# A two-layer transformer block on one core: hand-written entry lists for layer two's units 0 to 3, and the first expert-weight transfers beside slots 0 to 3

## The chip, the cores and the metric

The kernel runs on one core of one Trainium2 chip. The metric is the device time of one execution in microseconds; lower is better. The engines are TensorE (PE in the profile), VectorE (DVE), ScalarE (ACT), GpSimd (POOL) and SyncE (SP), each with an in-order list of instructions; they meet at semaphores.

## What is computed

The input x has 128 sequences of 64 tokens, 128 features each. Cut to its core, the reference is:

```python
x = x + tanh(g_xattn[0]) * xattn0(layernorm(x), ctx, ctx)   # 16 heads, mask by blocks of 32 keys
x = x + tanh(g_ffn[0])   * ffn0(layernorm(x))               # top-1 of 8 experts, gelu, 128 -> 512 -> 128
x = x + tanh(g_xattn[1]) * xattn1(layernorm(x), ctx, ctx)   # 16 heads, causal, key padding
x = x + tanh(g_ffn[1])   * ffn1(layernorm(x))
# ffn1: 16 experts, gates w = softmax over the active ones of (cosine(x, sim) - sigmoid(gates))
#   q, k, v = sum_e w_e * (x @ proj_e);  o = softmax(q k^T / sqrt(128)) v
#   out = sum_e w_e * (o @ o_proj_e)
```

## The kernel before, in words

The 8192 tokens are 32 units of 256 tokens (four sequences, two tiles of 128). Four stages follow each other: layer one's attention with its router, unit by unit (to about 384 us of the profile); the routing, which clears the padding rows and builds the slot table (384 to 398); layer one's experts, 71 slots of 128 sorted tokens (398 to 544); and layer two, attention and dense experts together (from 546 on).

Each engine's work is a list written out by hand. In layer two `body1(u)` is one step of the pipeline on each engine: it does the dense experts of unit u, the attention of unit u+2 (scores, maxima, subtraction, exponentials, transposes of the probabilities `upper_probs`, products with the values `upper_weigh`, heads, output), queries, keys and values of unit u+3 and the norm and first transposes `upper_in` of unit u+4. `upper_units` (L326) runs it for u = -5 to 33, so that for u below 0 only the parts of units that exist are there. The attention of unit 0 is thus in body1(-2) and that of unit 1 in body1(-1), one after the other in the same order as in the steady state. The step for u = 0 is the first with dense parts (L1758 to L1760, `part`).

What the change touches, with its lines:

- SP: `zero_rows` (L380) loads four row numbers into registers and then issues four transfers of zeros into `sorted_in`; ACT runs it too, for the other four experts. `load_slot` (L460) brings the rows of a slot. `load_context` (L488) brings a unit's stored context columns into `xcT`. `place_keys` (L404) spreads the keys `kT` into `kx` with four transfers.
- POOL: `gather` (L570) fetches a unit's tokens from `sorted_out` with two indirect transfers; `norm` and `second_norm` (L593 to L596, `deviation`) turn mean and variance into scale and shift; `pad_row` (L584, L587) makes a unit's mask; `add_part` (L718) adds the dense experts' parts.
- ACT: `apply_norm` (L812), `copy_xT` (L768), `keys` (L776), `queries` (L784), `copy_v` (L793), `exp_bank` (L911), `copy_pT` (L830), `copy_oT` (L837), `copy_hidden` (L918), `gate_exp` (L943), and `load_rows` (L892), which issues the transfers of the dense experts' weights `proj_raw`, two experts and one of q, k, v, o at a time.
- DVE: `first_stats` and `second_stats` (L1058 to L1062), `max_bank` (L1318), `normalise` (L1095, L1097), `add_residual` (L1104), and the gates (L1260 to L1310).
- PE: `upper_in` (L1853), `upper_queries_keys` (L1862 queries, L1863 keys), `upper_values` (L1523), `upper_scores` (masks L1887, products L1549), `subtract_bank` (L1896), `upper_probs` (L1569), `upper_weigh` (L1584), `upper_heads` (L1844), `upper_output` (L1872), `upper_normed` (L1819) and `gate_products` (L1827).

`upper_in`, `upper_values`, `upper_heads`, `upper_normed` and `gate_products` share the bank m0; queries, keys and output share m1; `since` names the semaphore after which the bank's earlier user is done.

Of the kernel before, what the change touches and what calls it, by code (L numbers as in the profile page):

```python
# [7 lines left out]
ACT = mybir.ActivationFunctionType  # L8
# [8 lines left out]
P = 128  # L17
# [9 lines left out]
RING0 = 6  # L27
# [50 lines left out]
def flamingo(nc, a, out):  # L78
    ctx = ExitStack()
    with ctx:  # L80
# [144 lines left out]
        with ExitStack() as first:  # L225
            def sb_first(name, shape):
# [60 lines left out]
                  "hn_lo_ready", "oh_lo_ready", "qk1_in_psum", "qk1_ready", "s1_in_psum",  # L287
# [38 lines left out]
        def upper_units(eng, body):  # L326

            for u in range(-5, UNITS + 2):
                body(u)
# [50 lines left out]
        def zero_rows(eng, experts):  # L380

            eng.wait_ge(routed["zero"], 1)
            rows = [eng.value_load(padi[0:1, e:e + 1], min_val=0, max_val=E0 * REGION - P) for e in experts]
            for row in rows:
                eng.dma_start(sorted_in[bass.ds(row, P), :], zrow[:, :]).then_inc(routed["padded"], 16)
# [5 lines left out]
        def _(sp):  # L391
# [78 lines left out]
            rows = [row_of(sl) for sl in range(2)]  # L470
            sp.wait_ge(routed["padded"], 16 * E0)
            for par in range(2):
                sp.wait_ge(scattered[par], 16 * UNITS)
            for sl in range(RING0):
                load_slot(sl, sl, rows[sl] if sl < 2 else row_of(sl))
            slots(sp, slot)

# [12 lines left out]

            def store(v):
# [10 lines left out]

            upper_units(sp, body1)
# [5 lines left out]
        def _(g):  # L509
# [228 lines left out]

            upper_units(g, body1)
# [3 lines left out]
        def _(act):  # L743
# [26 lines left out]
            def keys(layer, v):  # L770
                q = s[layer]
                if exists(v):
                    act.wait_ge(q["qk_in_psum"], v + 1)
# [102 lines left out]
            act.activation(warm[:, :], eps[:, :], ACT.Gelu)  # L876
            act.wait_ge(routed["table"], 1)
# [17 lines left out]

            def load_proj(i, n):
# [5 lines left out]
            for n in range(4):  # L902
                load_rows(slice(0, 2), n)
            slots(act, slot, load=load_proj)
# [100 lines left out]

            upper_units(act, body1)
# [3 lines left out]
        def _(v):  # L1010
# [437 lines left out]

            upper_units(v, body1)
# [3 lines left out]
        def _(pe):  # L1453
# [236 lines left out]
            ins.then_inc(setup["table_in_psum"], 1)  # L1690
            pe.wait_ge(routed["table"], 1)
# [164 lines left out]
            def upper_queries_keys(v):  # L1856

                if exists(v):
                    since((v - 4, f["qk1_ready"], v - 3), (v - 2, s[1]["x_mid_ready"], v - 1), (v - 1, s[1]["k_ready"], v))
                    pe.wait_ge(s[1]["xcT_ready"], v + 1)  # L1860
                    pe.wait_ge(ctx_loaded[1][v % 2], 8 * (v - v % 2 + 2))
                    pe.matmul(m1[:, 0:256], wq[1][:, :], xcT[v % 2][:, 0, :], start=True, stop=True)  # L1862
                    pe.matmul(m1[:, 256:512], wk[1][:, :], xcT[v % 2][:, 1, :], start=True, stop=True)\  # L1863
# [137 lines left out]
```

## Time and profile before

| | us |
|---|---|
| median of 3 runs | 1701.73 (1701.27 to 1704.68) |
| profiled execution, its own time | 1705.36 |
| its span from first to last instruction | 1703.6 |
| TensorE busy over the span | 1599.9 (94%) |
| last slot's output issued, first gather of layer two | 543.8, 546.4 |
| first dense part of layer two (L1758) | 601.5 |

The profile counts an instruction as busy between its start and its end; a row of the timeline gives start, duration, engine, line, operation, and in brackets how long the engine had been idle and what ended that. The chain of waits is followed back from the last instruction, so that each piece in it is what the end waited for. The granted clock of TensorE is written as a share of 2.4 GHz: 1.00 is 2.4 GHz and 0.50 is 1.2 GHz.

### The profile page before, as it was taken

What the parts mean: (1) busy time and instruction counts of PE and PEld (TensorE: products, weight loads), DVE (VectorE), ACT (ScalarE), POOL (GpSimd) and SP (SyncE); (2) the same over time, 40 slices, a digit from 0 to 9 for tenths busy, and PEclk for the clock granted to TensorE, in tenths of its full rate; (3) what the DMA queues carried; (4) which work ended last, traced back from release to release, by engine and by line L of the source; (5) the groups of instructions that cost most, each with busy time, mean ns of one, the idle gap of its engine ahead of it and who ended that gap; (6) DMA issues with size and microseconds to landing.
All of it is one profiled execution on the core that took longest, in us unless ns stands there. A gap on an engine that the chain in (4) does not pass through costs nothing.

```text
span 1703.6 us, 50846 instructions
## 1 busy us (share of the span) xinstructions
PE 1599.9 (94%) x15944; PEld 1395.1 (82%) x15945; DVE 1209.4 (71%) x3915; ACT 1079.5 (63%) x2724; POOL 1179.6 (69%) x1715
## 2 busy tenths in 40 slices
PE   6999999976997789999999999999999999999996
PEld 4777777756997578988888888988888899889885
DVE  3677777753554257888787878887878888877785
ACT  3777777743554446666666666676666666666654
POOL 3555555532454467888878887888788888887785
PEclk9999999987998689999999999999999999999998
DMA  3222222234542000000000000000000000000000
GB/s 85 95 74 74 74 74 74 70 99 119 144 133 77 28 12 14 20 15 17 17 20 14 17 17 20 14 17 17 20 14 17 17 19 15 17 17 11 5 8 10
DMA packets 92102, 68.95 MB, mean 40 GB/s; under 512 B 13937, under 2 KB 87697, under 8 KB 91921
## 3 DMA queue, kind: packets, MB, share of 16 engines
q1 hardware_dynamic: 76512, 49.34, 9.8%
q0 software_dynamic: 5120, 12.62, 2.3%
q10 hardware_dynamic: 10288, 4.74, 1.1%
q8 instruction: 94, 1.54, 0.4%
q14 instruction: 88, 0.71, 0.1%
HBM read 35.74 MB, written 22.52 MB: 34 GB/s over the span
## 4 chain that ended last, share of the span: by engine, by line
PE 84%; DVE 6%; issue 4%; POOL 3%; ACT 1%; DMA 1%; SPq 0%; DVEq 0%; POOLq 0%; ACTq 0%
PE s_bank L1758 13%; PE s_bank L1759 12%; PE s_bank L1760 12%; PE po L1584 8%; PE tb L1569 6%; PE s_bank L1700 4%; PE po L1712 4%; PE s_bank L1549 4%; PE s_bank L1896 2%; PE m L1523 1%; PE m L1610 1%; PE s_bank L1887 1%; PE tb L1758 1%; PE m L1508 1%; PE s_bank L1558 1%
## 5 line engine op out<-in xcount | busy, mean ns | idle before, releaser
L718 POOL TENSOR_TENSOR qkv<-qkv,scaled 128x384 f32<-128x384 f32 x480 | 490.6, 1022 | 135.8 <-ACT scaled L964 99.4
L964 ACT ACTIVATE scaled<-s_bank,wg 128x384 f32<-128x384 f32 x448 | 256.6, 582 | 128.6 <-PE s_bank L1760 127.0
L1758 PE MATMUL s_bank<-proj_hi,hn_hi 128*128 128x384 f32 x896 | 329.9, 368 | 1.1 <-DVE qkv L1364 0.9
L1364 DVE SCALAR_TENSOR_TENSOR qkv<-s_bank,wg,qkv 128x384 f32<-128x384 f32 x448 | 273.9, 611 | 48.9 <-PE s_bank L1760 37.2
L1759 PE MATMUL s_bank<-proj_lo,hn_hi 128*128 128x384 f32 x896 | 302.4, 337 | 0.0
L1760 PE MATMUL s_bank<-proj_hi,hn_lo 128*128 128x384 f32 x896 | 300.6, 335 | 0.0
L830 ACT ACTIVATE pT<-tb 128x512 f32<-128x512 f32 x256 | 152.1, 594 | 167.5 <-PE tb L1569 95.7
L1758 PEld LDWEIGHTS s_bank<-proj_hi,hn_hi 128*128 128x128 f32 x896 | 168.7, 188 | 16.0 <-ACT scaled L964 5.9
L1759 PEld LDWEIGHTS s_bank<-proj_lo,hn_hi 128*128 128x128 f32 x896 | 169.3, 189 | 2.9
L1760 PEld LDWEIGHTS s_bank<-proj_hi,hn_lo 128*128 128x128 f32 x896 | 168.3, 188 | 0.0
L1569 PE MATMUL tb<-ident,prob 128*128 128x128 f32 x1024 | 158.8, 278 | 5.1 <-ACT pT L830 5.1
L1584 PEld LDWEIGHTS po<-vb,pT 128*64 128x64 f32 x4096 | 141.5, 140 | 21.7 <-issue 21.7
L1584 PE MATMUL po<-vb,pT 128*64 128x18 f32 x4096 | 154.0, 214 | 0.4 <-ACT pT L830 0.4
L1375 DVE SCALAR_TENSOR_TENSOR halves<-s_bank,wg,halves 128x128 f32<-128x128 f32 x448 | 127.5, 344 | 24.6 <-DVE halves L1375 19.7
L1569 PEld LDWEIGHTS tb<-ident,prob 128*128 128x128 f32 x1024 | 119.0, 141 | 29.6 <-issue 20.0
L718 POOL TENSOR_TENSOR sums<-sums,scaled 128x512 f32<-128x512 f32 x96 | 123.4, 1286 | 12.0 <-ACT scaled L968 6.1
L911 ACT ACTIVATE prob<-s_bank 128x512 f32<-128x512 f32 x128 | 73.5, 600 | 84.1 <-PE s_bank L1896 84.1
L968 ACT ACTIVATE scaled<-s_bank,wg 128x128 f32<-128x128 f32 x384 | 109.6, 369 | 24.9 <-PE s_bank L1760 24.6
L886 ACT ACTIVATE hT<-s_bank,b_cols 128x128 f32<-128x128 f32 x284 | 81.1, 367 | 69.0 <-PE s_bank L1700 68.9
L1318 DVE TENSOR_REDUCE mx<-s_bank 128x8 fp32r<-128x512 f32 x128 | 79.5, 684 | 49.2 <-PE s_bank L1549 49.2
L641 POOL DMA_INDIRECT sorted_in<-xr,posi x64 | 66.1, 1033 | 67.4 <-DVE posi L1160 54.6
L1095 DVE RECIPROCAL rden<-po 128x32 f32<-128x32 f32 x64 | 22.9, 358 | 125.8 <-PE po L1584 125.8
(281 smaller groups left out, 3833.1 us busy)
## 6 DMA issues: line engine op xcount, KB each, us to landing
xs<-sorted_in SPq DMA_DIRECT2D x71, 128.5 KB, 2.1
kx<-kT SPq DMA_DIRECT2D x256, 32.0 KB, 1.8
sorted_out<-yo SPq DMA_DIRECT2D x71, 64.0 KB, 1.6
xin<-in_x SPq DMA_DIRECT2D x32, 128.0 KB, 2.1
cin<-in_ctx SPq DMA_DIRECT2D x32, 128.0 KB
ctx_cols<-xcT SPq DMA_DIRECT2D x32, 128.0 KB
w<-in_L_ffn_W SPq DMA_DIRECT2D x16, 256.0 KB, 3.7
xcT<-ctx_cols SPq DMA_DIRECT2D x32, 128.0 KB, 2.1
```

The costliest lines, as they stand in the source:

```text
L718: g.tensor_tensor(into, into, scaled[m % SCALED][:, 0:cols], ALU.add).then_inc(dense_added, 1)
L830: act.activation(pT[j % 2][:, :, :, :], tb[:, :].rearrange("p (r t n) -> p r t n", r=2, t=2), ACT.Copy).then_inc(q["probT_ready"], 1)
L886: ins = act.activation(hT[1 - par][:, cols], s_bank[1 - par][:, cols], ACT.Gelu, bias=b1_cols[:, bass.ds(e * FJ + j, 1)])
L964: ins = act.activation(into, bank[:, 0:3 * D], ACT.Copy, scale=wg[v % 4][:, 1, k:k + 1])
L968: ins = act.activation(part[:, cols] if k else sums[:, e, :], bank[:, cols], ACT.Copy, scale=wg[v % 4][:, 1, 4 * k + e:4 * k + e + 1])
L1364: v.scalar_tensor_tensor(out=acc, in0=bank[:, 0:3 * D], scalar=wg[w % 4][:, 0, k:k + 1], in1=acc, op0=ALU.mult, op1=ALU.add).then_inc(dens ...
L1375: ins = v.scalar_tensor_tensor(out=into, in0=bank[:, cols], scalar=wg[w % 4][:, 0, e:e + 1], in1=into, op0=ALU.mult, op1=ALU.add)
L1569: ins = pe.transpose(tb[:, col:col + P], prob[j][:, t, 2 * r:2 * r + 2, :], ident[:, :])
L1584: ins = pe.matmul(po[64 * half:64 * half + 64, col:col + 2 * VW], pT[j % 2][:, t, r, 64 * half:64 * half + 64], vb[par][:, seq, 2 * j + r, ...
L1758: pe.matmul(bank[:, 0:cols], hi[:, tile], of(proj_hi), start=True, stop=False)
L1759: pe.matmul(bank[:, 0:cols], hi[:, tile], of(proj_lo), start=False, stop=False)
L1760: pe.matmul(bank[:, 0:cols], lo[:, tile], of(proj_hi), start=False, stop=True)\
```

## The change

`upper_units` now starts at u = 0. What the five earlier steps did is written out as a list of its own on each engine, in an order of its own:

- Unit 0's keys are made during the routing stage: SP loads the context of units 0 and 1 before it waits for the zeros, PE multiplies unit 0's keys behind the slot table's transposes (new semaphore `first_keys`), ACT copies them ahead of its wait for the table, and SP places them behind the first six slot loads. `upper_queries_keys(0)` then has the queries only.
- POOL issues the gathers of units 0 and 1 back to back, ahead of unit 0's norm, and makes unit 0's mask and residual ahead of unit 1's norm.
- PE runs unit 0's scores directly behind its values, and unit 1's scores directly behind unit 0's last product with the values. Unit 0's heads, output and unit 2's `upper_in` follow within unit 1's subtractions. Products with the values alternate with the transposes of the probabilities.
- ACT copies unit 0's values ahead of unit 1's norm, and loads the table for Exp behind the last slot; `gate_exp(0)` stands ahead of unit 2's value copies and unit 1's `copy_oT`.
- `zero_rows` takes the four experts in two pairs: two register loads, two transfers, twice.
- The first four weight transfers, which ACT issued ahead of the slots, are issued behind slots 0, 1, 2 and 3.

```diff
@@ upper_units
-            for u in range(-5, UNITS + 2):
+            for u in range(UNITS + 2):
@@ zero_rows
-            rows = [eng.value_load(padi[0:1, e:e + 1], min_val=0, max_val=E0 * REGION - P) for e in experts]
-            for row in rows:
-                eng.dma_start(sorted_in[bass.ds(row, P), :], zrow[:, :]).then_inc(routed["padded"], 16)
+            for pair in (experts[0:2], experts[2:4]):
+                rows = [eng.value_load(padi[0:1, e:e + 1], min_val=0, max_val=E0 * REGION - P) for e in pair]
+                for row in rows:
+                    eng.dma_start(sorted_in[bass.ds(row, P), :], zrow[:, :]).then_inc(routed["padded"], 16)
@@ sync: the block from rows = ... to slots(sp, slot) moved behind load_context's definition
+            load_context(0)
+            load_context(1)
             rows = [row_of(sl) for sl in range(2)]
             sp.wait_ge(routed["padded"], 16 * E0)
...
             for sl in range(RING0):
                 load_slot(sl, sl, rows[sl] if sl < 2 else row_of(sl))
+            place_keys(1, 0)
             slots(sp, slot)
...
+            load_context(2)
+            place_keys(1, 1)
+            load_context(3)
+            place_keys(1, 2)
+            load_context(4)
             upper_units(sp, body1)
@@ gpsimd
+            gather(0)
+            gather(1)
+            norm(1, 0)
+            pad_row(0)
+            residual(1, 0, 0)
+            norm(1, 1)
+            pad_row(1)
+            gather(2)
+            residual(1, 1, 1)
+            norm(1, 2)
+            gather(3)
+            hidden_norm(0)
+            hidden_length(0)
+            norm(1, 3)
+            lower_hidden(0)
+            residual(1, 2, 0)
+            pad_row(2)
+            hidden_norm(1)
+            gather(4)
+            hidden_length(1)
             upper_units(g, body1)
@@ scalar
+                    if layer == 1 and v == 0:
+                        act.wait_ge(f["first_keys"], 1)
...
             act.activation(warm[:, :], eps[:, :], ACT.Gelu)
+            keys(1, 0)
             act.wait_ge(routed["table"], 1)
...
+            def first_slots(sl, n, par, rnd):
+                slot(sl, n, par, rnd)
+                if isinstance(sl, int) and 0 <= sl < 4:
+                    load_rows(slice(0, 2), sl)
...
-            for n in range(4):
-                load_rows(slice(0, 2), n)
-            slots(act, slot, load=load_proj)
+            slots(act, first_slots, load=load_proj)
+            act.activation(warm[:, :], eps[:, :], ACT.Exp)
...
+            apply_norm(1, 0, 0)
+            copy_xT(0)
+            queries(1, 0)
+            copy_v(q, 0, 0)
+            apply_norm(1, 1, 1)
+            copy_xT(1)
+            exp_bank(0, 0)
+            keys(1, 1)
+            exp_bank(0, 1)
+            queries(1, 1)
+            copy_pT(q, 0, 0)
+            exp_bank(0, 2)
+            copy_pT(q, 0, 1)
+            exp_bank(0, 3)
+            copy_v(q, 1, 1)
+            copy_pT(q, 0, 2)
+            copy_pT(q, 0, 3)
+            apply_norm(1, 2, 0)
+            copy_oT(q, 0)
+            exp_bank(1, 0)
+            copy_xT(2)
+            exp_bank(1, 1)
+            copy_pT(q, 1, 0)
+            exp_bank(1, 2)
+            exp_bank(1, 3)
+            copy_pT(q, 1, 1)
+            apply_second_norm(1, 0, lambda t: x3[0][:, t, :], lambda t: hn[:, t, :])
+            copy_pT(q, 1, 2)
+            copy_hidden(0)
+            copy_pT(q, 1, 3)
+            queries(1, 2)
+            keys(1, 2)
+            gate_exp(0)
+            copy_v(q, 2, 0)
+            copy_oT(q, 1)
+            apply_norm(1, 3, 1)
+            copy_xT(3)
+            apply_second_norm(1, 1, lambda t: x3[1][:, t, :], lambda t: hn[:, t, :])
             upper_units(act, body1)
@@ vector
+            first_stats(1, 0, 0)
+            first_stats(1, 1, 1)
+            for j in MAXIMA:
+                max_bank(0, j)
+            first_stats(1, 2, 0)
+            normalise(s[1], 0)
+            for j in MAXIMA:
+                max_bank(1, j)
+            add_residual(1, 0, 0, x3[0][:, :, :])
+            second_stats(1, 0, x3[0])
+            first_stats(1, 3, 1)
+            gates = Steps(v, f["gate_steps"], 0, GATE)
+            gate_norm(0, gates)
+            gate_logits(0, gates)
+            gate_top(0, gates)
+            normalise(s[1], 1)
+            gate_index(gates)
+            gate_shift(gates)
+            gate_mask(gates)
+            add_residual(1, 1, 1, x3[1][:, :, :])
+            gate_softmax(0, gates, wg[0])
+            second_stats(1, 1, x3[1])
             upper_units(v, body1)
@@ tensor
             ins.then_inc(setup["table_in_psum"], 1)
+            pe.wait_ge(ctx_loaded[1][0], 16)
+            pe.matmul(m1[:, 256:512], wk[1][:, :], xcT[0][:, 1, :], start=True, stop=True).then_inc(f["first_keys"], 1)
             pe.wait_ge(routed["table"], 1)
...
+            upper_in(0)
+            upper_queries_keys(0)
+            upper_values(0)
+            upper_scores(-2)
+            upper_in(1)
+            for j in SUBTRACTED[0:2]:
+                subtract_bank(0, j)
+            pe.wait_ge(s[1]["qk_ready"], 1)
+            upper_queries_keys(1)
+            for j in SUBTRACTED[2:4]:
+                subtract_bank(0, j)
+            upper_probs(0, 0)
+            upper_values(1)
+            upper_probs(0, 1)
+            upper_weigh(0, 0)
+            upper_probs(0, 2)
+            upper_weigh(0, 1)
+            upper_probs(0, 3)
+            upper_weigh(0, 2)
+            upper_weigh(0, 3)
+            upper_scores(-1)
+            upper_heads(0)
+            subtract_bank(1, SUBTRACTED[0])
+            pe.wait_ge(s[1]["qk_ready"], 2)
+            upper_output(0)
+            subtract_bank(1, SUBTRACTED[1])
+            upper_in(2)
+            for j in SUBTRACTED[2:4]:
+                subtract_bank(1, j)
+            upper_probs(1, 0)
+            upper_probs(1, 1)
+            upper_weigh(1, 0)
+            upper_probs(1, 2)
+            upper_weigh(1, 1)
+            upper_normed(0)
+            upper_probs(1, 3)
+            upper_weigh(1, 2)
+            upper_queries_keys(2)
+            gate_products(0)
+            upper_weigh(1, 3)
+            upper_values(2)
+            upper_heads(1)
+            upper_output(1)
+            upper_in(3)
             upper_units(pe, body1)
```

## Rows read from the trace of the kernel before

**Rows 1.** Busy time, share and instructions of each engine, from the page.

```profile
PE 1599.9 (94%) x15944; PEld 1395.1 (82%) x15945; DVE 1209.4 (71%) x3915; ACT 1079.5 (63%) x2724; POOL 1179.6 (69%) x1715
```

**Rows 2.** Windows: stretch, length, PE, PEld, DVE, ACT, POOL busy, clock, DMA share, GB/s.

```profile
563.00:580.00 17.00, 12.73 (x143) 9.52 (x142) 3.91 (x10) 7.79 (x16) 4.76 (x9) 0.70 0.08 25
580.00:602.00 22.00, 18.44 (x165) 14.18 (x165) 9.19 (x39) 9.13 (x23) 8.60 (x17) 0.58 0.06 20
602.00:636.00 34.00, 29.20 (x255) 25.44 (x254) 18.97 (x58) 17.45 (x38) 23.88 (x34) 0.90 0.04 13
```

**Rows 3.** Chain of waits through the routing stage: start, duration, what.

```profile
385.00 0.48 SPq L383
...
387.72 0.36 SPq L385
...
389.33 6.53 DMA sorted_in<-zrow
396.02 2.06 DMA xs<-sorted_in
```

**Rows 4.** The two queues, SP's q1 and ACT's q10, in 393 to 395 us.

```profile
q10 hardware_dynamic: 646, 0.32, 91.6%
q1 hardware_dynamic: 88, 0.08, 32.9%
```

**Rows 5.** Timeline of SP and ACT around the first slots and weight transfers.

```profile
396.02 5.27 SPq L460 DMA_DIRECT2D xs<-sorted_in  x6
406.31 0.35 SPq L466 DMA_DIRECT2D sorted_out<-yo  x1
...
410.34 1.14 ACT L886 ACTIVATE hT<-s_bank,b_cols 128x128 f32<-128x128 f32 x4 [0.76 <-PE s_bank L1700]
...
417.43 0.41 ACTq L892 DMA_DIRECT2D proj_raw<-in_L_ffn_k_proj  x1
```

**Rows 6.** Chain of waits from layer two's first gather to the first maxima.

```profile
546.38 1.15 POOL xin L570
...
551.17 0.26 DVE mv L1062 x2
...
555.33 2.59 DMA xin<-sorted_out,placei
...
560.63 0.89 ACT xn L812 x2
...
565.30 1.30 DVE mx L1318 x2
```

**Rows 7.** Timeline of PE in layer two's entry.

```profile
556.25 1.06 PE L1863 MATMUL m<-xcT,wk 128*128 128x256 f32 x2
557.24 1.12 PE L1523 MATMUL m<-wv,xcT 128*64 128x64 f32 x16
...
575.25 1.92 PE L1584 MATMUL po<-vb,pT 128*64 128x18 f32 x32
578.17 0.66 PE L1844 MATMUL m<-ident,on 128*128 128x128 f32 x2 [1.01 <-DVE on L1097]
579.40 1.20 PE L1872 MATMUL m<-wo,oT 128*128 128x128 f32 x4 [0.56 <-ACT oT L837]
...
580.96 1.04 PE L1887 MATMUL s_bank<-identb,mask_keys 64*128 64x256 bf16 x8
581.92 2.01 PE L1549 MATMUL s_bank<-kx,qT 32*64 32x256 f32 x32
```

**Rows 8.** Timeline: the first dense part, POOL's last adds, its reader.

```profile
601.50 0.67 PE L1758 MATMUL tb<-proj_hi,hn_hi 128*128 128x384 f32 x1
...
630.11 5.56 POOL L718 TENSOR_TENSOR qkv<-qkv,scaled 128x384 f32<-128x384 f32 x5
...
635.82 1.09 PE L1780 MATMUL m<-ident,qkv 128*128 128x128 f32 x4 [3.62 <-POOL qkv L718]
```

**Rows 9.** Who waited for whom, 540 to 602 us: total, times, longest.

```profile
ACT pT L830 <- PE po L1584: 4.4, 2, 2.3
```

## What is predicted, and from what

> **What bounds the kernel now.** First the page: TensorE is busy for 94% of the span [rows 1], so nothing is to be had where it streams, and the other engines' shares say nothing by themselves. What counts is where TensorE idles or runs at half clock, and the busy time by window shows two such places that the change touches. In the routing stage, from 388 to 396 us, nothing computes. In layer two's entry TensorE is busy for 12.73 of 17 us and 18.44 of 22 us, at a mean granted clock of 0.70 and 0.58, which is a mixture of the levels 2.4 and 1.2 GHz [rows 2]. The chain of waits then names what holds each place. In the routing stage it is the last transfer of zeros, 6.53 us from issue to landing, and behind it the first slot's load, 2.06 us [rows 3]. In the entry it is a row of hand-overs: the gather of unit 1's tokens, its norm, unit 0's scores, the maxima [rows 6], then unit 0's attention to its end and, only behind that, unit 1's scores [rows 7]. The first dense part starts at 601.50 [rows 8]. In the first dense step the chain ends on GpSimd's adds: five of them in 5.56 us, and TensorE waits 3.62 us for the last [rows 8]. That step's list is unchanged, so it should move as a whole.
>
> **The zeros and the slots' start.** Register loads and issues per queue start at 385.00 and end with the fourth issue near 389.7: two groups of four [rows 3]. In pairs the count is the same, so the last zeros are issued at the same time; the first two go about 1.1 us earlier, by two of the four register loads, which with their pauses fill 385.00 to 387.72. The transfers are limited by the DMA engines: between 393 and 395 the ACT queue holds 91.6% of them with 646 packets, those of the weight transfers issued from 389.8 on, while SP's last 88 packets are still under way [rows 4]. With the weights gone, those 88 packets have the engines to themselves. I take 1.3 us for that and 1.1 us for the earlier start, together 2.4 us of the 6.53. New in SP's queue are two context transfers, 128 KB each like the weight transfers but in half the packets; they stand behind the zeros and ahead of the first slot's rows. If they delay those by a third of a slot load (2.06 us), 0.6 us go again. Sum: 1.8 us. The bounds are 0, if zeros written to DRAM are slow by themselves, and 3.4 us, if the last zeros land as fast as an undisturbed load, 2.1 us plus 1 us behind their issue at 389.33 instead of 6.53 behind it.
>
> The Trainium skill has a rule here (DMA: Bandwidth & Descriptors, "Queues, rings and completion order"): each DMA engine takes turns between the queues, packet by packet. By it alone SP's zeros would have had half of each engine all along and could gain no more than the other half for the few packets left; the row with 88 of 734 packets agrees, and the sum would be 1.1 plus some 1.0 less 0.6, or 1.5 us.
>
> **What this adds beside the slots.** Unit 0's key product on TensorE waits for its context; queued behind it are the wait for the table and the first slot's transpose, which now waits until 398.2 for its rows, later than the context in the same queue, so I cost it at nothing. ACT's key copy (0.47 us) stands ahead of its first gelu at 401.4: nothing. SP places the keys behind six slot loads of 5.27 us and ahead of the first store at 406.31 [rows 5]; it has about 5 us for four issues of 0.6 us: nothing, and 2.4 us at most if the context is late. The four weight issues cost ACT's sequencer about 0.41 us each; in the rounds that already have them they overlap the running gelus, and ACT idles 0.76 us ahead of a slot's gelus [rows 5]. Nothing; if they did stretch slots 0 to 3 it would be four times 0.4, 1.6 us. The Exp table load of 1.28 us moves from a place where ACT waited anyway to one where it waits for the gather: nothing.
>
> **Unit 0 to its scores.** Its gather, landing and statistics are unchanged, to 551.4 [rows 6]. But GpSimd issues unit 1's gather in front of unit 0's norm. One gather is two instructions of some 1.1 us [rows 6]; with their pauses unit 0's goes from 546.4 to 548.9, and unit 1's would follow until about 551.9. That costs the norm 0.5 us. The keys' product leaves the path, 1.06 us at this clock [rows 7], of which I count 1.0. The scores stand right behind the values, which end at 558.36 (557.24 + 1.12): 558.36 + 0.5 - 1.0 = 557.9. Mask (1.33 us of GpSimd) and keys are there by then. Before, the masks' product started only at 562.1, because unit 1's first transposes stood ahead and waited for a gather whose second half was issued only at 555.3 [rows 6]. Scores take 3.0 us at 1.2 GHz (580.96 to 583.93, rows 7), half of that at 2.4. The first maximum comes at 561.1 at the low clock and 559.8 if the clock rises as it did at this point before. I take 560.7 against 565.30 [rows 6]: 4.6 us ahead.
>
> **Unit 0 to its last product.** From first maximum to last product with values it is now 11.9 us (565.30 to 577.17, rows 6 and 7), on the same instructions. Handing the products over one by one saves a wait or two: worked out piece by piece it comes to 11.9 us with everything at 1.2 GHz and 9.7 us at 2.4 GHz. The windows show 0.70 here [rows 2], and I take 11.2. That ends at 571.9, 5.3 us ahead.
>
> **Unit 1's scores** need the exponentials of unit 0, done long before, and keys that SP places about 4 us after their copy near 565. They start at 571.9 instead of 580.96: 9.1 us ahead, as normalisation, heads, output and unit 2's transposes (577.17 to 580.96) no longer stand ahead of them.
>
> **Unit 1's scores to the first dense part.** Part of that comes back. It takes 20.5 us now (580.96 to 601.50) and has to take in unit 0's heads 0.66, output 1.20 and unit 2's transposes 0.6 [rows 7]. With every product at the low clock, from the scores' start: scores end 3.0; heads and first maximum 3.7; first subtraction 4.1; output 5.5; second subtraction 6.0; unit 2's transposes 6.6; two subtractions 7.6; first probabilities 8.2; a copy, second ones 9.5; product 10.4; third ones and second product 12.2; unit 0's hidden transposes 12.9; fourth ones 13.5; third product 14.4; queries and keys of unit 2 16.1; gate products 16.7; last product 17.6. Then a new wait: unit 1's heads reuse the bank of unit 2's values, ACT's copy of these (0.8) stands behind `gate_exp(0)`, and that waits on VectorE for normalisation (0.8), index and shift (0.8); with 0.2 for the exponential the heads start at 20.4 instead of 18.4. Heads 0.7, copy 0.5, output 1.2 and unit 3's transposes 0.6: 23.4. So dense starts at 571.9 + 23.4 = 595.3, 6.2 us ahead. I count 6.0, as the hand-made chain leaves out some hand-overs of 0.1 us. Bounds: 4.5 (low clock throughout, 596.5, and half a microsecond of hand-overs) and 8.5 (2.4 GHz up to unit 0's last product).
>
> Everything that the first dense step needs is ahead by as much: unit 2's scores, `gather(4)` behind unit 1's second norm, the weights of the gates. Sum: 1.8 + 6.0 = 7.8 us. The profiled execution took 1705.36 us, 1.76 outside its span of 1703.6, and is 3.6 above the median of 1701.73; differences carry over to the median: 1693.9 us.
>
> **Rivals.** (a) The entry hands most back. The new order binds ACT: copies, exponentials and waits in one file, with the wait on the gates at its end. For it: ACT's transposed-probability copies already wait up to 2.3 us for products [rows 9], and in the sum above 3 of 9 us are already lost. Against it: ACT is busy for 9.13 of 22 us [rows 2]. If half of eight such copies come 0.9 us later each, the entry gives 2.5 us and the whole 4.3 or less: 1698.5, down to no entry gain at all at 1700. (b) More clock: with fewer gaps TensorE stays at 2.4 GHz through unit 1 too; the 18.44 us of products at 0.58 [rows 2] would give some 3 us more: 1690.5. Against it: of the two windows the busier one has the lower clock [rows 2]. The Trainium skill (TensorE: Matmul & The Clock Gate, "The HAM clock gate") says that a busy array gets the full clock and an idle one loses it; the trace agrees only in part, by the same two windows. (c) The change doesn't do what it says: if unit 0's start were held by its own gather alone and unit 1's by the gates, only the start of the slots would move: 1699.9. (d) Slower: ACT's file order turns against it, each of the eight copies of transposed probabilities waiting behind an exponential or norm for the longest such wait seen, 2.3 us [rows 9], TensorE standing each time: 18 us against a gain of 7.8, or 1712. It decides from 1.0 us a copy, where the gain is gone, and is slower by over 0.2% from 1.4 us. I find no piece of the chain with such a wait.
>
> **How the numbers follow.** Forecast 1693.9 with its own range of 1691.5 to 1697: 0.58. (b) 0.13. (a) 0.16, (c) 0.08, (d) 0.05. The bounds of the terms give 1701.73 - 8.5 - 3.4 = 1689.8 and 1701.73 - 4.5 - 0 = 1697.2. The range of 1689.5 to 1699.5 adds the better half of (a) and leaves out (c), (d) and the ends. A measurement of this kernel tells 0.2%, 3.4 us, from no change: faster means under 1698.3. That is the forecast, (b) and part of (a): 0.80. Same 0.15, slower 0.05.
>
> **What would show it.** The last zeros land near 393.5 and the first slot's transpose starts near 396.4. Counted from the first gather: unit 0's first maximum 14.3 us behind it instead of 18.9, unit 1's scores 25.5 instead of 34.6, the first dense part 49 instead of 55.1. ACT's `gate_exp(0)` shows a wait on VectorE and TensorE idles about 2 us ahead of unit 1's heads. The first dense step stays at 34.3 us (601.50 to 635.82). If that step grows, the gain went to GpSimd's adds [rows 8]; if unit 1's scores are ahead by 9 us but the dense part is not by 6, it went to ACT's order. Wrong would be the whole if the slots' period changed or the steady state behind it.

## The result: about twice the forecast gain

| | before | changed |
|---|---|---|
| median of 4 runs, us | 1703.20 (1701.27 to 1704.85) | 1690.24 (1685.81 to 1690.68) |
| profiled execution, us | 1705.36 | 1690.68 |
| its span, us | 1703.6 | 1689.0 |
| first gather to first dense part | 55.12 | 40.46 |
| tokens' counts (`padi`) to first slot's transpose | 13.42 | 12.60 |

The changed kernel takes 0.9916 of the time of before, with an interval of 0.9904 to 0.9929. On 1703.2 us that is 14.3 us, 12.1 to 16.4. The forecast was 7.8 us. The direction was right and so were the hand-overs that the new order removes, but the size was not: 1690.24 lies at the very edge of the range, and the ratio applied to the median that the forecast started from, 1701.73, gives 1687.4, below it.

TensorE's busy time is what it was (94%), as in [rows 1]:

```profile
PE 1590.5 (94%) x15944; PEld 1388.4 (82%) x15945; DVE 1208.1 (72%) x3915; ACT 1079.9 (64%) x2725; POOL 1179.0 (70%) x1715
```

The two traces, stage by stage. The count of tokens is ready at 384.80 before and 387.35 after: 2.55 us lost in layer one, which the change doesn't touch; over the ten executions on this kind of chip that point lies anywhere from 382.9 to 387.8, so it is noise. From there to the first slot's transpose 0.8 us are gained, in the slots nothing, in the entry 14.66 us, in the first dense step 0.90 us (34.32 to 33.42), in all that follows 0.8. Together: -2.55 + 0.8 + 0.05 + 14.66 + 0.90 + 0.8 = 14.7 us of span.

The entry of the changed kernel by window: first gather to unit 0's scores, to unit 1's scores, to the first dense part; then the first dense step. Columns as in [rows 2].

```profile
548.06:559.19 11.13, 2.84 (x20) 1.73 (x21) 1.47 (x8) 1.73 (x4) 9.38 (x16) 0.50 0.09 24
559.19:571.55 12.36, 10.21 (x148) 7.33 (x146) 3.22 (x8) 8.63 (x19) 6.99 (x10) 0.94 0.19 55
571.55:588.52 16.97, 12.57 (x170) 9.56 (x167) 8.52 (x37) 9.30 (x23) 6.37 (x15) 0.98 0.05 17
...
588.52:621.94 33.42, 28.62 (x256) 25.49 (x255) 19.80 (x63) 17.57 (x38) 23.71 (x33) 0.96 0.05 13
```

The clock column is what the forecast missed. Before, it stood at 0.70 and 0.58 in the entry [rows 2]; now at 0.94 and 0.98, that is 2.4 GHz nearly throughout, behind a first part at 1.2 GHz (0.50). From unit 1's scores to the dense part alone it was 0.58 before and is 0.98 now. The timeline of TensorE shows the same at single products: the 16 value products took 1.12 us for unit 0 at the low clock, as before [rows 7], but 0.69 us for units 1 and 2, and the output products 0.61 us instead of 1.20 [rows 7].

```profile
558.13 1.12 PE L1621 MATMUL m<-wv,xcT 128*64 128x64 f32 x16
...
571.55 0.61 PE L1989 MATMUL s_bank<-identb,mask_keys 64*128 64x256 bf16 x8
...
574.47 0.61 PE L1974 MATMUL m<-wo,oT 128*128 128x128 f32 x4
...
583.62 0.69 PE L1621 MATMUL m<-wv,xcT 128*64 128x64 f32 x16
586.44 0.44 PE L1944 MATMUL m<-ident,on 128*128 128x128 f32 x2 [2.14 <-ACT vb L825]
```

The last line is the wait that the change adds, and that the forecast named: unit 1's heads wait 2.14 us for unit 2's value copies, behind the exponential of the gates.

### The profile page after: what moved, and what is told of

Its sections match the earlier page's. It is cut to its first block, busy times and chain, and to the rows that moved or that the text cites. A ratio compares the mean times of both kernels' runs of the same rounds, so it can differ in the third digit from the quotient of the medians.

```text
span 1689.0 us, 50848 instructions
## 1 busy us (share of the span) xinstructions
PE 1590.5 (94%) x15944; PEld 1388.4 (82%) x15945; DVE 1208.1 (72%) x3915; ACT 1079.9 (64%) x2725; POOL 1179.0 (70%) x1715
## 4 chain that ended last, share of the span: by engine, by line
PE 84%; DVE 6%; issue 4%; POOL 2%; ACT 1%; DMA 1%; SPq 1%; DVEq 0%; POOLq 0%; ACTq 0%
PE s_bank L1858 13%; PE s_bank L1859 12%; PE s_bank L1860 12%; PE po L1682 8%; PE tb L1667 6%; PE s_bank L1800 4%; PE po L1812 4%; PE s_bank L1647 4%; PE s_bank L1998 2%; PE m L1621 1%; PE m L1708 1%; PE s_bank L1989 1%; PE tb L1858 1%; PE m L1606 1%; PE s_bank L1656 1%
```

## The experiments

There are two main theories. **Order**: the lists shorten the path itself, at any clock. **Clock**: the lists also close the gaps, TensorE is granted 2.4 GHz, and that is the surplus. Beside them stand smaller questions: K, whether placing unit 0's keys stood on the path; W, the wait on the gates; S, the zeros and weights.

The kernels ran in four sets, each on one chip with runs of the kernel before beside it. The chips differ: the kernel before takes 1808.7 and 1804.0 us in the first two sets, 1701.4 and 1703.4 in the last two. Ratios are to before in the same set. The times below are of the one profiled execution each, counted from the first gather: unit 0's first maximum, the masks' product of unit 1's scores, the first dense part, and the mean clock over the whole entry.

| kernel | set | ratio (interval) | max | scores 1 | dense | clock |
|---|---|---|---|---|---|---|
| before | first | 1 | 18.92 | 34.58 | 55.12 | 0.62 |
| changed | first | 0.9916 (0.9904, 0.9929) | 13.61 | 23.49 | 40.46 | 0.84 |
| zeros_and_weights_only | 1 | 0.9984 (0.9968, 0.9999) | 19.18 | 34.72 | 55.29 | 0.62 |
| entry_lists_only | 1 | 0.9959 (0.9944, 0.9975) | 14.99 | 25.30 | 43.77 | 0.78 |
| keys_in_the_entry | 1 | 0.9978 (0.9962, 0.9994) | 17.89 | 29.85 | 48.35 | 0.71 |
| before_with_filler | 1 | 0.9988 (0.9974, 1.0002) | 18.97 | | 50.06 | 0.93 |
| changed_again | 2 | 0.9933 (0.9920, 0.9947) | 14.97 | 26.63 | 45.10 | 0.76 |
| value_copies_first | 2 | 0.9937 (0.9924, 0.9950) | 14.93 | 26.61 | 43.65 | 0.77 |
| scores_behind_output | 2 | 0.9986 (0.9974, 0.9998) | 14.91 | 30.67 | 53.67 | 0.63 |
| changed_with_filler_ahead | 2 | 0.9909 (0.9894, 0.9925) | 11.74 | 21.63 | 39.46 | 0.96 |
| filler_and_value_copies | 3 | 0.9918 (0.9900, 0.9936) | 11.67 | 21.55 | 37.17 | 1.00 |
| scores_behind_output_filled | 3 | 0.9958 (0.9943, 0.9974) | 11.66 | 24.42 | 45.89 | 0.82 |
| gather_behind_norm | 3 | 0.9956 (0.9939, 0.9973) | 14.58 | 25.97 | 43.38 | 0.74 |
| keys_in_the_entry_filled | 3 | 0.9976 (0.9962, 0.9989) | 17.28 | 28.32 | 45.13 | 0.92 |
| changed_third | 4 | 0.9927 (0.9909, 0.9946) | 13.49 | 23.38 | 40.34 | 0.84 |
| filler_ahead_second | 4 | 0.9911 (0.9890, 0.9932) | 11.68 | 21.56 | 38.98 | 0.96 |
| filler_and_copies_second | 4 | 0.9894 (0.9873, 0.9915) | 11.80 | 21.67 | 37.29 | 1.00 |
| old_order_filled_second | 4 | 0.9973 (0.9961, 0.9985) | 18.91 | | 49.78 | 0.90 |

### The parts apart

zeros_and_weights_only is the kernel before with:

```diff
-            rows = [... for e in experts]
+            for pair in (experts[0:2], experts[2:4]):
...
-            for n in range(4):
-                load_rows(slice(0, 2), n)
-            slots(act, slot, load=load_proj)
+            slots(act, first_slots, load=load_proj)
```

> The kernel before with two parts of the change alone: the zeros in pairs of experts, and the first four weight transfers behind slots 0 to 3. My forecast put 2.4 us on this without the two context transfers. The two traces say less: from the count of tokens per expert (the padi row) to the first slot's transpose it is 13.42 us before and 12.60 us in the changed kernel, so with the context transfers 0.8 us. Theory S (the start of the slots gives little): 0.5 to 1.5 us faster, last zeros landing 5 to 6 us behind their issue. Rival: the zeros' landing is bound by the writes themselves, whatever stands beside them: 0 +- 0.5 us, landing 6 us or more behind the issue.

entry_lists_only is the changed kernel with these two taken back.

> The changed kernel with the zeros in fours and the first weight transfers ahead of the slots again; the entry's lists and unit 0's early keys stay. If nearly all of the gain is the entry's, it stays 11 to 14 us faster than before and the first dense part lies 40 to 41 us behind the first gather, as in the changed kernel (40.5) against 55.1 before. If the zeros and weights carry more than their trace shows, it is under 10 us faster. The context of unit 0 now stands beside 512 KB of weights: the key product could come 1 to 2 us later, and the first slot with it.

The zeros and weights give 0.16%, 2.9 us, with an interval that ends at zero (0.2 to 5.8 us), so the kernel's time doesn't tell S from its rival. The lists alone give 0.41%, 7.4 us, where the whole change (changed_again) gave 0.67% in the next set, on the same kind of chip. That misses the 11 to 14 us expected, and the dense part comes at 43.77 us and not at 40 to 41: I had taken both from the first kind of chip, and on this kind the changed kernel itself has 45.10. The two intervals just touch, and 0.41% and 0.16% together come near the whole.

From the count of tokens to the first slot's transpose it is 13.42 and 13.05 us with zeros in fours on the first kind of chip, and 12.50 us as the mean of eight executions in pairs (11.97 to 13.08). So this part is worth 0.7 us there. On the other kind it is 14.72 and 13.74 against 12.33 to 13.38, or 1 to 2 us. In the changed kernel the chain is:

```profile
392.44 5.26 DMA sorted_in<-zrow
397.86 1.96 DMA xs<-sorted_in
```

The last zeros still land 5.26 us behind their issue, with no weight transfer beside them (the two context transfers stand behind them), against 6.53 [rows 3]. The first issue comes 1.7 us behind the count instead of 2.9, as forecast (1.2 us). But the last one comes 5.09 us behind it instead of 4.53, as the second pair waits for its own register loads, and the landing is only 0.7 us earlier by the count (10.35 instead of 11.06 us).

The first set can part pairs from weights, with one execution each. In entry_lists_only ACT's copy of unit 0's keys stands ahead of the weight issues, so that these came only 12.8 us behind the count, and its zeros in fours had no weights beside them. Counted from the tokens' count, the last zeros land at 12.33 us in fours with weights (before_with_filler, 7.81 us behind the issue), at 11.31 us in fours without (entry_lists_only, 6.79), and at 10.24 us in pairs without (zeros_and_weights_only, 5.22). There the weights cost some 1.0 us and the fours 1.1. On the first kind of chip both together give 0.7 us, within executions in pairs that differ by 1.1 us; no run there parts them.

### Unit 0's keys

keys_in_the_entry takes the early keys back: no product in the routing stage, and in the entry

```diff
-                    if v > 0:
+                    if True:
                         ins = pe.matmul(m1[:, 256:512], wk[1][:, :], xcT[v % 2][:, 1, :], ...)
@@ scalar
             queries(1, 0)
+            keys(1, 0)
             copy_v(q, 0, 0)
@@ sync
-            place_keys(1, 0)
             slots(sp, slot)
+            place_keys(1, 0)
             load_context(2)
```

> The changed kernel, but unit 0's keys are multiplied, copied and placed in the entry again, behind its queries. My forecast cost this part at 1.0 us, the product alone. Theory K (the placing was on the path too): scores then wait for product, copy and four transfers, of which the trace of before shows 557.7 for the copy's start to about 563 for the last landing; first maximum 5 to 6 us later, the kernel 4 to 6 us slower than the changed one (7 to 9 us faster than before). Forecast's view: 1 us slower than the changed kernel. If the longer gap also takes the 2.4 GHz clock away in the part that follows, it is 7 to 10 us slower than the changed one.

keys_in_the_entry_filled adds 11 products ahead of the entry:

```diff
+            pe.wait_ge(setup["pad_keys"], 1)
+            keep_busy(tb, 512, 11)    # products ident x b2b that nobody reads
             upper_in(0)
```

> Unit 0's keys in the entry again, with the 11 products ahead of it. Without them the same order took 48.35 us from first gather to dense against 43.8 and 45.1 with early keys. Theory K (placing is on the path): the first maximum stays 3 us or more behind that of the changed kernel with filler (11.7 us), at 15 us or more, as transfers don't run on TensorE's clock. Rival (the loss was the clock): first maximum within 1.5 us, at 13.2 us or less.

The first maximum comes 2.9 us later without filler (17.89 against 14.99 in entry_lists_only) and 5.6 us later with it (17.28 against 11.68 in filler_ahead_second), the dense part 4.6 and 6.2 us against the same two. The 2.9 us are fewer than the 5 to 6 expected: on that kind of chip the first maximum comes at 15.0 us even with early keys, not at 13.5 as on the first (last section). Theory K holds: the price is the placing, which didn't get shorter with TensorE's clock. Once the product goes at 2.4 GHz the wait is all the more visible:

```profile
555.04 2.42 SPq L405 DMA_DIRECT2D kx<-kT  x4
...
559.54 2.02 PE L1644 MATMUL s_bank<-kx,qT 32*64 32x256 f32 x32 [4.25 <-DMA kx<-kT]
```

TensorE stands 4.25 us for the keys, and the products behind run at the low clock again (2.02 us instead of 1.12).

### The clock in the old order and in the new

before_with_filler and old_order_filled_second are one kernel, the one before with:

```diff
+                if u in (-2, -1):
+                    keep_busy(po, 256, 1)
                 upper_probs(u + 2, 1)
...
+                if u == -2:
+                    keep_busy(po, 256, 1)
                 upper_probs(u + 2, 2)
...
+                if u in (-2, -1):
+                    keep_busy(tb, 256, 1)
                 upper_heads(u + 2)
...
+                if u == -4:
+                    pe.wait_ge(setup["pad_keys"], 1)
+                    keep_busy(tb, 512, 11)
+                if u == -3:
+                    keep_busy(s_bank[0], 256, 5)
                 upper_in(u + 4)
```

> The kernel before, its order unchanged, with TensorE kept busy in the entry's waits by products that nobody reads: 11 of 128x512 ahead of the entry, 5 of 128x256 ahead of unit 1's first transposes, and single ones ahead of second and third probabilities and of the heads. Clock theory: what made the changed entry 14.7 us shorter instead of 6.0 is that its products ran at 2.4 GHz; then the old order at 2.4 GHz gains too, as some 20 us of half-clock products on its path (563 to 602) halve in part: first dense part 46 to 50 us behind the first gather instead of 55.1, the kernel 5 to 9 us faster. Rival (order alone, the hand-made chain was mis-sized elsewhere): the clock rises but the entry stays within 2 us of 55.1.

> The kernel before with filler in the entry's waits. The old order at 0.90 or more: entry 49 to 51 us; the difference to the filled new order, 10 to 12 us, is the order's own; the kernel 0.25 to 0.5% faster than before. If the clock is what carried the change, it comes within 5 us of the changed kernel.

changed_again and changed_third are the changed kernel; changed_with_filler_ahead and filler_ahead_second are it with the 11 products ahead of `upper_in(0)`.

> The changed kernel once more, beside the variants of this set. Entry from first gather to first dense part 40 to 44 us at a mean clock of 0.78 to 0.85; 11 to 14 us faster than the kernel before on the same chip if that chip is like the first, 7 to 10 us if it is like the second one.

> The changed kernel again, as the base of this set. Order theory (the order gives 10 to 11 us at any clock, the clock up to 5 more): entry 40 to 45.5 us depending on the clock granted, the kernel 0.65 to 0.85% faster than before.

> The changed kernel with 11 products of 128x512 that nobody reads on TensorE ahead of the entry, in its 11 us of idle time. Clock theory: the first 5 us of the entry, which ran at 1.2 GHz (5 us of products, 555.8 to 560.7), run at 2.4 GHz: first maximum 1.5 to 2.2 us earlier, entry 38 to 39 us, the kernel 1.5 to 2.5 us faster than the changed one. Rival (what follows waits on ACT and the clock is high by itself): first maximum earlier, but the dense part by less than 0.7 us.

> The changed kernel with the 11 products ahead of the entry. Clock theory: entry 37.5 to 39.5 us at 0.95 or more, 1 to 5 us under the changed kernel's in the same set, and the kernel 0.1 to 0.25% faster than it. Rival: no difference beyond 0.1%, as the dense stage gives it back.

Both theories hold, side by side. The old order takes 55.1 to 55.3 us at 0.62 and 49.8 to 50.1 at 0.90 to 0.93: the clock is worth 5.2 to 5.3 us to it, and more in its first dense step, which falls from 34.3 to 33.0 on the first kind of chip and from 36.0 to 33.0 on the other. Most of it is one stretch, from unit 1's scores to the dense part: 20.57 us at 0.58 (zeros_and_weights_only) and 16.31 at 1.00 (before_with_filler, same set):

```profile
639.49:655.80 16.31, 11.83 (x163) 8.95 (x163) 8.89 (x39) 8.72 (x21) 8.62 (x17) 1.00 0.09 27
```

The filler itself costs the path nothing: in before_with_filler TensorE still waits for another engine behind each piece of it, 0.34 to 2.62 us.

The whole kernel gains less than these 7 and 8 us: 0.27% (4.6 us, 2.6 to 6.6) and 0.12% (2.2 us). In the two traces of the first kind of chip 2.05 us of it are lost in layer one, which is the same in both, and 0.5 us behind the first dense step. On the other kind I haven't found where the rest goes.

The new order takes 39.0 and 39.5 us with the filler. So at a high clock in both (0.96 against 0.90 and 0.93) the order alone is worth 10.6 to 10.8 us. That is more than the 6.0 us of the forecast; what it would be worth with both at the low clock no run shows. The changed kernel without filler got 40.3 to 45.1 us: at 0.84 in two executions on the first kind of chip, at 0.76 in the one on the other, where the first maximum also comes 1.5 us later (last section). Unit 1's scores to the dense part, first in changed_again, then in filler_ahead_second:

```profile
628.00:646.47 18.47, 14.12 (x167) 10.44 (x167) 8.30 (x37) 9.25 (x22) 6.37 (x15) 0.87 0.05 16
```

```profile
570.13:587.55 17.42, 13.02 (x169) 10.08 (x167) 8.30 (x37) 9.30 (x23) 7.39 (x16) 0.92 0.09 25
```

### The order of unit 1's scores

scores_behind_output puts one stretch of TensorE's list back:

```diff
-            upper_scores(-1)
             upper_heads(0)
-            subtract_bank(1, SUBTRACTED[0])
             pe.wait_ge(s[1]["qk_ready"], 2)
             upper_output(0)
-            subtract_bank(1, SUBTRACTED[1])
             upper_in(2)
+            upper_scores(-1)
+            subtract_bank(1, SUBTRACTED[0])
+            subtract_bank(1, SUBTRACTED[1])
```

> The changed kernel with unit 1's scores on TensorE behind unit 0's heads, output and unit 2's first transposes, as in the kernel before. Theory O (order): TensorE waits there for normalisation and two copies, some 3.8 us before; the products behind take the saved 2.5 us (or 1.3 us at 2.4 GHz) off again, so the entry is 2.5 to 3.5 us longer than the changed one at the same clock. Clock theory adds to it: the four us with gaps take 2.4 GHz away from what follows, mean clock from scores to dense under 0.8, entry 5 to 8 us longer.

It is the dearest single piece: dense at 53.67 instead of 45.10, 8.6 us (0.6 over what order and clock together were expected to cost), and the ratio falls back to 0.9986. Unit 1's scores start 4.0 us later, and from there the same products take 23.0 instead of 18.5 us at 0.57, though heads, output and transposes are now out of that window:

```profile
628.84:651.84 23.00, 18.75 (x160) 13.95 (x159) 7.63 (x35) 9.05 (x21) 6.34 (x15) 0.57 0.04 12
```

To part the two, scores_behind_output_filled has the 11 products ahead, and

```diff
+            keep_busy(tb, 256, 2)
             upper_heads(0)
             pe.wait_ge(s[1]["qk_ready"], 2)
+            keep_busy(tb, 256, 1)
             upper_output(0)
```

> Unit 1's scores behind unit 0's output, as in the variant that lost 8.6 us of the entry, but with products that nobody reads: 11 of 128x512 ahead of the entry, 2 of 128x256 ahead of unit 0's heads, 1 ahead of its output. Clock theory: most of the 8.6 us was the clock (mean 0.57 from unit 1's scores to the dense part against 0.87); with it near 1.0 the entry takes 42 to 44 us, that is 2.5 to 4 us over the 39.5 of the changed order with filler, the price of the order alone. Order theory: the late scores cost 7 us or more at any clock, entry 46 us or more.

Up to unit 1's scores, at 1.00 in both, the order costs 2.8 us (24.42 against 21.55 to 21.67). Then my filler failed: 2.4 GHz ended at about 578.1, behind unit 1's subtractions. In TensorE's timeline four transposes of probabilities take 0.66 us, and the next four, 1.4 us later, 1.08; the rest ran at 1.2 GHz (second fence, the window from unit 1's scores to the dense part, mean 0.62).

```profile
573.49 1.12 PE L1647 MATMUL s_bank<-kx,qT 32*64 32x256 f32 x32
575.54 2.27 PE L1998 MATMUL s_bank<-mx,minus_ident 128*128 128x512 f32 x4 [0.93 <-DVE mx L1394]
577.65 0.66 PE L1667 MATMUL tb<-ident,prob 128*128 128x128 f32 x4
579.09 1.08 PE L1667 MATMUL tb<-ident,prob 128*128 128x128 f32 x4 [0.78 <-ACT pT L862]
```

```profile
572.95:594.42 21.47, 17.25 (x159) 13.18 (x159) 7.61 (x35) 9.05 (x21) 6.31 (x15) 0.62 0.05 14
```

The 45.89 us lie between both expectations and decide for neither over the whole entry. Nor are 2.8 us the price of the order: heads, output and transposes are then done, and some of it comes back behind the scores; how much, no run shows at a like clock. Why the clock fell there, behind 4.5 us without a wait and one wait of 0.93 us, is open.

### Two small pieces

value_copies_first:

```diff
-            gate_exp(0)
             copy_v(q, 2, 0)
+            gate_exp(0)
```

> The changed kernel with ACT's copies of unit 2's values ahead of gate_exp(0). Theory W (the wait on the gates at the end of ACT's list stands on the path, as forecast at 2 us, while the trace of the changed kernel shows 2.14 us of TensorE idle ahead of unit 1's heads): the copies start at the end of the values, 584.3 instead of 585.6, and the dense part starts 1.0 to 1.3 us earlier: 1 us faster than the changed kernel. Rival: the heads then wait for normalisation (584.8) and everything behind shifts less than 0.5 us.

The heads' wait falls from 2.14 us (in the changed kernel on the first kind of chip) to 0.91 and the entry is 1.45 us shorter than in changed_again, as theory W has it, though its last part also ran at 0.90 instead of 0.87; in the kernel's time it doesn't show (0.9937 against 0.9933).

```profile
642.07 0.44 PE L1944 MATMUL m<-ident,on 128*128 128x128 f32 x2 [0.91 <-ACT vb L825]
```

gather_behind_norm puts `gather(1)` behind `norm(1, 0)` on GpSimd.

> The changed kernel with unit 1's gather behind unit 0's norm on GpSimd, as before. Forecast's view: unit 0's norm comes 0.5 us earlier (0.3 by the trace of the changed kernel: GpSimd free at 553.16, statistics at 553.15), unit 1's tokens land some 1.9 us later but are needed only behind the scores: entry 0 to 0.5 us shorter. Rival: unit 1's norm comes later than the scores' end and TensorE waits for its transposes: entry 1 to 3 us longer.

My view was wrong and the rival right: dense at 43.38 against 40.3 to 40.5. The gather now stands ahead of unit 0's mask and the masks' product waits for it; unit 1's norm then comes late, and TensorE waits for it in the middle of unit 0's maxima. The clock was 0.72 in that part against 0.94 in the changed kernel, so the late mask and norm are not all of the 3 us: the products of the scores took 2.01 us instead of 1.30.

```profile
556.61 1.03 PE L1989 MATMUL s_bank<-identb,mask_keys 64*128 64x256 bf16 x8 [0.32 <-POOL mask_keys L596]
...
560.33 0.66 PE L1953 MATMUL m<-ident,xn 128*128 128x128 f32 x2 [0.75 <-ACT xn L844]
```

### A faster version

filler_and_value_copies and filler_and_copies_second are one kernel: the changed one with the 11 products ahead of the entry, the value copies first, and `keep_busy(s_bank[0], 256, 1)` ahead of `upper_heads(1)`.

> The changed kernel with the 11 products ahead of the entry, the value copies ahead of gate_exp(0), and one more product of 128x256 ahead of unit 1's heads. The two parts gave 5.6 us (filler) and 1.5 us (copies) in single executions. Clock theory and theory W add: entry 37.5 to 39 us against 39.5 with the filler alone, the kernel 5 to 7 us faster than the changed one and some 17 us faster than before. Rival: both shorten the same wait and the sum is no better than the filler alone.

> Filler ahead of the entry and of unit 1's heads, value copies first. Entry 37 to 38 us; the kernel 0 to 0.1% faster than with the filler ahead alone, 0.15 to 0.35% faster than the changed one.

The entry is at 2.4 GHz from end to end and takes 37.2 and 37.3 us:

```profile
569.60:585.22 15.62, 12.97 (x172) 9.70 (x169) 8.47 (x37) 9.40 (x23) 7.25 (x16) 1.00 0.06 16
```

In the set that has the changed kernel too, its median is 1687.29 us against 1691.76, 4.5 us less, and 1.06% less than before (0.9894) against 0.73%. The intervals of the two ratios still overlap slightly, so the 4.5 us are likely and not certain. In the third set the same kernel gave 0.82% (0.9918), 14 us and not the 17 expected. With the filler ahead alone the kernel was 0.24% and 0.16% faster than the changed one, again with overlapping intervals.

## Why the prediction was right in direction and half in size

- **The zeros and the slots' start: 1.8 us forecast, 0.8 measured** (0.7 over eight executions). The first issue came earlier as costed, but the last came 0.56 us later, where I had it unchanged; and of the 1.3 us for the weights' share of the DMA engines nothing shows on this kind of chip, though the first set has 1.0 us for it. [Rows 4] showed the weights beside the last zeros, and I took being together for being slowed. The turns that the Trainium skill describes (DMA: Bandwidth & Descriptors, "Queues, rings and completion order") would have left 1.5 us here; the trace shows less than that too, and no run here shows how the engines took turns. The low end of the term, 0, was nearer than its top, 3.4.
- **Beside the slots: right.** First gather behind the first slot's transpose: 148.16 before, 148.11 after. Early keys, weight issues and placing are hidden.
- **Unit 0 to its first maximum: 4.6 us forecast, 5.3 measured** (18.92 to 13.61). Right on the whole. The 0.5 us that the second gather should have cost the norm was mis-sized: the normalized tokens begin 6.75 us behind the first gather (554.81 - 548.06) where it was 6.70 (553.08 - 546.38), so it costs 0.05. The 1.0 us for the keys counted their product alone. Had they been left in the entry, their placing would have cost 5.6 us (keys_in_the_entry_filled). Before, it was hidden: the last keys landed at 562.43, just ahead of the products at 563.11, while TensorE waited for unit 1's norm and ran the masks.
- **Unit 0 to its last product: 11.2 us forecast, 9.9 measured** (561.67 to 571.55). It ran at 0.94; I had worked out 9.7 us for 2.4 GHz and leaned to the low end.
- **Unit 1's scores to the dense part: 23.4 us forecast, 16.97 measured.** This is the step that failed, with 6.4 of the 8.7 us that the entry gave over its 6.0. The term was worked out with every product at 1.2 GHz, since that was the clock of this stretch before [rows 2], and the changed kernel ran it at 0.98. But the clock of a stretch is a result of the order, not a property of the stretch. What the clock is worth there the old order shows, 20.57 us at 0.58 and 16.31 at 1.00, 4.3 us; the changed list at the low clock was not run, so how the 6.4 us divide between clock and the hand-made chain stays open. The waits were named rightly: the one on the gates is there, 2.14 us against 2.0 forecast.
- **Nothing in the first dense step: 0.9 us measured** (34.32 to 33.42), again the clock, 0.96 against 0.90 [rows 2].
- **The rivals.** (b), more clock, had the mechanism and its 1690.5 was the best number, with some luck: it put 3 us on the clock, which was worth 5.2 to 5.3 us to the old order's entry, and 1693.9 - 3 is 1690.9. I gave it 0.13, with the argument that of two windows the busier one had the lower clock. The Trainium skill's rule (TensorE: Matmul & The Clock Gate, "The HAM clock gate") that an idle array loses the full clock and a busy one gets it is borne out by the filler runs, 0.62 to 0.90 and 0.76 to 0.96, and not plainly by scores_behind_output_filled, where it fell behind a wait of 0.93 us. I should have weighed it more. (a), (c) and (d) did not happen: ACT's file held. The number of (a) was added wrongly: a whole gain of 4.3 us gives 1697.4, not 1698.5.
- **The bound.** 8.5 us for the entry took 2.4 GHz only up to unit 0's last product, and 14.66 were measured. At 2.4 GHz to its end the last part of the new order takes 16.82 us (keys_in_the_entry_filled, 1.00), where the bound still had 23.4.

Open stay: what decides the clock within the changed entry (0.84, 0.84, 0.76 in three executions), and so how the 14.3 us divide in each run; with filler as the yardstick, 10.6 to 10.8 us of the entry are the order's and the rest, 4 us in the first trace, the clock's. Also open is the order's share in what the place of unit 1's scores was worth (8.6 us with the clock).

## What to carry to other kernels

When a list of work is reordered on an engine with a granted clock, cost the new stretch at both clocks to its end, and forecast from the gaps that the new order leaves, not from the clock that the old one had. In the lead-in of a pipeline, put the next unit's independent work right behind the last product of the one before, instead of keeping the steady state's order; and take whatever depends on transfers alone (here keys and their placing, 5.6 us) into an earlier stage. Idle time of TensorE that lies ahead of such a stretch can be filled with products that nobody reads, if their number is fitted to the gap; here that gave 0.16 and 0.24% of the kernel's time, near the noise.

## What the hardware showed that was not expected

- On the chips of the first two sets the kernel before takes 1800 to 1814 us, against 1696 to 1708. Products and exponentials there take the same time each (medians of 0.374 and 0.597 us on the first kind, 0.374 and 0.598 on the other), but VectorE waits for the products of the scores: in a steady-state step of before_with_filler the maxima start 3.01 us behind VectorE's last work, with nothing in the profile that ends the wait, while the last score product ended 1.9 us earlier; on the first kind of chip VectorE starts 0.2 us behind that product. In the first maximum of changed_again it is 1.5 us. In the changed entry that delays the first maximum from 13.5 to 15.0 us. The cause is open.

```profile
801.66 1.89 DVE L1318 TENSOR_REDUCE mx<-s_bank 128x8 fp32r<-128x512 f32 x3 [3.01 <-remote]
```

- Products that nobody reads, 11 of 128x512 in the idle time ahead of the entry, kept 2.4 GHz from the first gather on and took 1.8 us off the first maximum (13.49 to 11.68). The entry is 1.4 us shorter by it in the fourth set; the first dense step took 33.97 us instead of 33.55, at 0.90 instead of 0.96.
